# Feed-forward inputs of a fused transformer layer: normalised one step earlier and turned by transfers and VectorE

## What is computed

```python
x = x + LN(ffn(LN(x)))
# ffn: gu = x @ ternary(w_gate_up).T; gate, up = split(gu)
#      h = silu(gate) * up;  hn = h / sqrt(mean(h*h) + eps);  return hn @ ternary(w_proj).T
```

## Time and profile before

| | |
|---|---|
| median of 3 runs | 1040.49 us (1040.42 to 1040.52) |
| the profiled execution | 1039.91 us, span 1038.1 us |
| busy, share of the span | PE 98%, PEld 95%, DVE 80%, ACT 84%, POOL 90% |
| granted TensorE clock | 0.997 of full speed |
| transfers | 56 GB/s over the span, 17.2% of the 16 DMA engines' time |

### The profile page before, as it was taken

How to read it: one execution, slowest core, us unless ns; L and a number is a source line. 1 busy time by engine, 2 the same in 40 slices (tenths; PEclk the granted TensorE clock), 3 DMA queues, 4 the chain that set the end, 5 groups by cost and what they waited for, 6 DMA issues and landing times.

```text
span 1038.1 us, 25078 instructions
## 1 busy us (share of the span) xinstructions
PE 1021.4 (98%) x7827; PEld 981.6 (95%) x7827; DVE 827.1 (80%) x2841; ACT 868.2 (84%) x2399; POOL 931.4 (90%) x926
## 2 busy tenths in 40 slices
PE   7999999999999999999999999999999999999996
PEld 6899999999999999999999999999999999999996
DVE  6868888878887888788888888887777767677776
ACT  5988898989898989898989898889898867877774
POOL 4899999999999999999999999999999847877775
PEclk9999999999999999999999999999999999999998
DMA  7561121112112110121122112111131000000001
GB/s 262 187 184 43 42 63 41 43 52 68 44 36 61 63 42 33 62 63 42 33 68 67 42 39 75 43 42 53 42 113 31 2 1 11 22 24 29 22 22 41
DMA packets 35124, 58.56 MB, mean 56 GB/s; under 512 B 3136, under 2 KB 16000, under 8 KB 34688
## 3 DMA queue, kind: packets, MB, share of 16 engines
q1 hardware_dynamic: 34992, 56.96, 17.2%
HBM read 50.92 MB, written 9.18 MB: 58 GB/s over the span
## 4 chain that ended last, share of the span: by engine, by line
POOL 60%; PE 19%; issue 14%; DVE 1%; POOLq 0%; ACT 0%; ACTq 0%; DVEq 0%
POOL arena L599 15%; POOL arena L622 14%; POOL arena L633 13%; POOL arena L609 13%; PE psum L1017 12%; PE psum L1057 6%; POOL arena L581 1%; POOL arena L557 1%; POOL X L590 1%; PE psum L775 1%; PE psum L1030 1%; POOL arena L565 0%; PE psum L1039 0%; POOLq L303 0%; POOL arena L572 0%
## 5 line engine op out<-in xcount | busy, mean ns | idle before, releaser
L633 POOL TENSOR_TENSOR arena<-arena 128x768 f32<-128x768 f32 x128 | 196.2, 1533 | 8.9 <-DVE arena L1580 8.3
L609 POOL TENSOR_TENSOR arena<-arena 128x512 f32<-128x512 f32 x128 | 174.0, 1359 | 10.0
L1593 DVE SCALAR_TENSOR_TENSOR pt_split<-psum,vh_col,pt_split 128x256 fp32r<-128x256 f32 (+1 forms) x512 | 177.0, 407 | 3.5 <-ACT pt_split L1252 3.0
L599 POOL TENSOR_TENSOR arena<-arena,tables 128x512 f32<-128x512 f32 x128 | 166.9, 1304 | 13.7 <-ACT arena L1222 13.0
L622 POOL TENSOR_TENSOR arena<-arena 128x512 f32<-128x512 f32 x127 | 162.9, 1283 | 0.0
L929 PE MATMUL psum<-arena 128*128 128x256 f32 x512 | 153.9, 382 | 3.1 <-POOL arena L609 1.8
L775 PE MATMUL psum<-wo_hi,o_hi 128*128 128x256 f32 x512 | 152.1, 297 | 0.0
L1233 ACT ACTIVATE arena<-arena 128x256 f32<-128x256 f32 x256 | 128.6, 502 | 26.7 <-DVE arena L1570 20.1
L775 PE MATMUL psum<-xt_lo,wq_hi 128*128 128x256 f32 x512 | 144.7, 283 | 0.0
L775 PE MATMUL psum<-xt_hi,wq_lo 128*128 128x256 f32 x512 | 144.5, 282 | 0.0
L775 PE MATMUL psum<-wo_hi,o_lo 128*128 128x256 f32 x512 | 144.3, 282 | 0.0
(11 more groups left out here) (195 smaller groups left out, 3405.7 us busy)
## 6 DMA issues: line engine op xcount, KB each, us to landing
arena<-kh_rows SPq DMA_DIRECT2D x127, 256.0 KB, 3.3
out<-spare SPq DMA_DIRECT2D x15, 256.0 KB, 2.1
arena<-w_rows SPq DMA_DIRECT2D x6, 512.0 KB, 4.8
X<-L_attn_Wout SPq DMA_DIRECT2D x1, 2048.0 KB, 14.5
X<-L_attn_x SPq DMA_DIRECT2D x1, 2048.0 KB, 12.5
arena<-L_attn_Wq SPq DMA_DIRECT2D x1, 1536.0 KB, 10.0
X<-L_attn_x SPq DMA_DIRECT2D x1, 1536.0 KB, 9.7
w_rows<-L_ffn_w_gate_up SPq DMA_DIRECT2D x3, 512.0 KB, 8.2
```

Of the source, the lines that this page charges most:

```text
L599: nc.gpsimd.tensor_tensor(swap, swap, spread, ALU.mult).then_inc(q_sined, 1)
L609: nc.gpsimd.tensor_tensor(q_rot[p % 2], q_cos[p % 2], q_swap[p % 2], ALU.add).then_inc(q_roped, 1)
L633: nc.gpsimd.tensor_tensor(tb, tb, r.unsqueeze(3).to_broadcast([P, HP, 3, P]), ALU.mult).then_inc(p_ready, 1)
L1593: last = nc.vector.scalar_tensor_tensor(pt_lo[p % 2][:, o], b[:, i], vh[:, t, h:h + 1], pt_hi[p % 2][:, o].bitcast(F32), ALU.mult, ALU.sub ...
```

## The change

The normalising moves from a unit's second step to its first (FLAG norm=0), behind `square_hidden` 2 on ScalarE. TensorE's `turn_x2` goes for all units but unit 0. In its place SyncE issues four SBUF to SBUF transfers of 64 KB each, which spread the blocks over the partitions, and VectorE does one 32x32 block transpose of 128x512 float32 into F_BANK. ScalarE's `split_x2` moves ahead of `activate` 2, and VectorE's ahead of `stats_x2`, which itself stays in its step. SyncE's loop of stores is unrolled, and the transfers of unit u+4 stand behind the store of unit u. A new buffer `moved` of 2 KB in each partition is used.

```diff
-FLAG = dict(stats=0, norm=1, turn=1, up=2, sum=3, down=3, z=3, out=4)
+FLAG = dict(stats=0, norm=0, turn=1, up=2, sum=3, down=3, z=3, out=4)
+        moved = sb("moved", [P, NT * E])
+        by_rows = lambda rows, t: rows.rearrange("p t e -> p (t e)").rearrange("p (b k t c) -> p t k b c", b=4, k=ET, t=NT)[:, t]
+        by_blocks = lambda x_tile: x_tile.rearrange("p (k b c) -> p k b c", k=ET, b=4)
+        moved_in = moved[:, :].rearrange("p (a g c) -> p g a c", a=4, c=P // 4)
+        turned_out = F_BANK.rearrange("p (g q a) -> p g a q", a=4, q=P // 4)
...
 # SyncE
+            def spread_blocks(rows, landed):
+                flat = rows.rearrange("p t e -> p (t e)")
+                for b in range(4):
+                    sp.dma_start(moved[b * 32:(b + 1) * 32, :].rearrange("q (a g) -> q a g", a=4),
+                                 flat[:, b * P:(b + 1) * P]).then_inc(landed, 16)
...
-            with sp.Fori(0, BATCH - 3, 2) as u:
-                for i in range(2):
-                    rows = out_rows[:, bass.ds(address((u + i) * NT), NT), :]
-                    sp.wait_ge(res_done, u + i + 1)
-                    sp.dma_start(rows, res[i]).then_inc(stored[i], 16)
+            def move_x2(u):
+                sp.wait_ge(x2_norm, u * NT + NT)
+                sp.wait_ge(x2_turned, u)
+                spread_blocks(x2_rows(u, u % 2), x2_moved)
+            for u in range(1, 4):
+                move_x2(u)
+            for u in range(BATCH - 2):
+                sp.wait_ge(res_done, u + 1)
+                sp.dma_start(out_rows[:, u * NT:(u + 1) * NT, :], res[u % 2]).then_inc(stored[u % 2], 16)
+                if u + 4 < BATCH:
+                    move_x2(u + 4)
...
 # TensorE, step
                 at = unit_at(u0, s, FLAG["turn"])
-                if at and at[0] > 0:
-                    turn_x2(*at)
...
 # ScalarE, norm_x2
-                    nc.scalar.activation(x2_rows(u, i)[:, t, :], x_batch(u)[:, t, :], ACT.Identity, bias=x2_bias[:, t:t + 1],
+                    o, i_ = x2_rows(u, i)[:, t, :], x_batch(u)[:, t, :]
+                    if u > 0:
+                        o, i_ = by_rows(x2_rows(u, i), t), by_blocks(i_)
+                    nc.scalar.activation(o, i_, ACT.Identity, bias=x2_bias[:, t:t + 1],
...
 # VectorE
+            def turn_x2(u):
+                dve.wait_ge(x2_moved, u * 64)
+                dve.wait_ge(x2_lo_done, u)
+                nc.vector.transpose(turned_out, moved_in).then_inc(x2_turned, 1)
```

More of the change, by code:

```diff
@@ L284, in sandwich_kernel @@
         wgu_placed, wpr_placed = sem("wgu_placed"), sem("wpr_placed")
+        x2_moved = sem("x2_moved")
         x2_stats, x2_aggr, x2_eps, x2_neg, x2_inv, x2_biased, x2_norm, x2_turned, x2_hi_done, x2_lo_done = (
@@ L1338, in step @@
                     activate(*at, 1)
+                at = unit_at(u0, s, FLAG["up"])
+                if at:
+                    high_hidden(*at, 1)
+                    square_hidden(*at, 0)
+                    square_hidden(*at, 1)
+                at = unit_at(u0, s, FLAG["turn"])
+                if at and at[0] > 0:
+                    split_x2(*at)
+                at = unit_at(u0, s, FLAG["up"])
+                if at:
+                    activate(*at, 2)
+                    high_hidden(*at, 2)
+                    activate(*at, 3)
+                    square_hidden(*at, 2)
                 at = unit_at(u0, s, FLAG["norm"])
@@ L1343, in step @@
                 if at:
[L1344 to L1355, removed]
                     high_hidden(*at, 3)
@@ L1767, in step @@
                     multiply(*at, 1)
+                at = unit_at(u0, s, FLAG["turn"])
+                if at and at[0] > 0:
+                    turn_x2(at[0])
                 at = unit_at(u0, s, FLAG["z"])
@@ L1778, in step @@
                     multiply(*at, 2)
-                at = unit_at(u0, s, FLAG["turn"])
-                if at and at[0] > 0:
-                    split_x2(*at)
                 at = unit_at(u0, s, FLAG["z"])
```

## The result

The changed kernel takes **1067.67 us** (median of 6 runs, 1066.96 to 1071.67) against 1040.51 (6 runs, 1040.3 to 1040.53) before: ratio 1.0272, 95% interval 1.026 to 1.0283 (the two medians alone give 1.0261). It is slower by 27.2 us. The forecast was slower by 5.8 us, with a range that ended at 1054.5. The profiled execution took 1071.03 us around a span of 1069.2, 3.4 above the median. Its first norm_x2 starts at 766.55, where the kernel before has 763.92: its stream is 2.6 us late already ahead of the feed-forward part, and I take those 2.6 us out where I compare starts.

What follows compares the result with a forecast made beforehand. TensorE was taken to bound the kernel at 12.17 us a step, then a ring through SyncE at 12.85. Start +1.3, ten steps +6.8 and end -2.3 gave +5.8 us: 1046.3 us, range 1040.0 to 1054.5.

Steps and rivals of the forecast that it cites:

- What bounds before, and direction: Feed-forward part: TensorE alone sets the old step of 12.17 us; the change makes the kernel slower, chance 0.76.
- a ring through SyncE's queue: Blocked steps: transpose to add_x, store, four issues, landing, next transpose; 12.85 us a step (12.4 to 13.4), chance 65%.
- The new order at 12.28 us: ScalarE and VectorE: the moved operations need 12.28 us a step even with every transfer in time.
- The transpose at 0.70 us: VectorE: the new 32x32 block transpose takes 0.70 us, with bounds of 0.61 and 1.29.
- The rival of the dear transpose: VectorE: strided PSUM writes make the transpose take 1.3 us, the step 13.45 us and the total 1052.9 us; chance 14%.
- The ring inside the engines, 9.43 us: VectorE and GpSimd: from the start of the transpose to the end of add_x takes 9.43 us.
- The way through SyncE, 3.42 us: SyncE: from add_x through store, four issues and the fourth landing to the transpose takes 3.42 us (3.0 to 4.0).
- The early steps, "at nothing": Steps where SyncE's transfers are not behind a store: no net cost, TensorE's gain of 3 x 0.44 taken by the longer ring.
- The first blocked steps, +1.3: First steps with transfers behind a store: stats_z falls 1.3 us later, as leftovers of attention hold GpSimd anyway.
- The end, -2.3: Step after unit 15's transpose, without norm_x2, stats_x2 and invert_x2: about 9.8 us instead of 12.16, so -2.3 us.
- the transfers come in time: Rival: transfers land within 2.85 us of add_x, so ScalarE's and VectorE's order sets 12.28 us a step; 1039.8 us, chance 14%.
- TensorE stayed the bound: Rival: the engines' ring closes in under 11.73 us, so all 15 turns taken from TensorE are won; 1033.9 us, chance 7%.

Runs made afterwards that it cites:

- moves_first: The changed kernel with SyncE issuing the transfers of unit u+4 ahead of the store of unit u: 1044.99 us.
- stats_behind: stats_early with the four transfers put back behind the store on SyncE: 1061.55 us.
- no_moves: The changed kernel without its transfers; VectorE transposes the normalised rows where they lie, blocks not spread: 1044.14 us.
- split_back: moves_first with ScalarE's split_x2 back behind activate 2 and VectorE's back behind multiply 2: 1039.18 us.
- plain_moves: The changed kernel with its four transfers as plain copies of 32 rows of 2 KB to the same partitions, blocks not spread: 1065.09 us.
- stats_early: moves_first with the input's statistics a step earlier, norm_x2 back behind activate 1 and both split_x2 at their old places: 1035.86 us.
- stats_only: moves_first with only the input's statistics a step earlier (FLAG stats=-1), norm_x2 left at its late place: 1073.32 us.

## Why the prediction was wrong, step by step

**What bounds before, and direction.** Right. The time won on TensorE was lost to a ring through SyncE's queue; moves_first shows it by its removal, stats_behind by its return.

**The new order at 12.28 us.** Right: 12.27 in moves_first and 12.27 to 12.28 in no_moves, with high 2 idle 1.95 us. In split_back, where split_x2 is back, it is 11.9.

**The transpose at 0.70 us.** Right: 0.73, and its slot to stats_z 0.63 (954.91 to 955.54). The rival of the dear transpose falls, and with it the fear for a strided write: the Trainium skill, "SBUF — State Buffer", "Door 1: The DMA port swizzle", warns of non-contiguous access to PSUM for matmuls, and this write of VectorE at a stride of four elements takes 0.04 us more than VectorE's product of 128x512 (0.69).

**The ring inside the engines, 9.43 us.** Right: transpose to the end of add_x is 962.95 + 1.29 - 954.91 = 9.33 us in the base steps. In three steps (those from 897.36, 911.68 and 982.82) it was 9.6 to 9.8.

**The way through SyncE, 3.42 us. This is the term that failed, and the largest of the misses.** It takes 4.6 us (964.24 to 968.85), outside even my upper bound of 4.0:

| part | predicted | measured |
|---|---|---|
| store and three issues, to the start of the fourth | 1.80 | 2.39 (964.24 to 966.63) |
| landing of the fourth | 1.60 | 2.20 |

Both were read from the nearest rows, and in both the row was another kind of transfer. The 0.42 us came from output stores; an issue of this kind takes 0.60, and next to next 0.65 (965.33 to 965.99). For the landing I interpolated by size between 16 KB and 256 KB, but at 64 KB these land like the store of 256 KB (2.1), as does a single copy of 256 KB (2.4). The Trainium skill, "DMA: Bandwidth & Descriptors", "Anatomy of one DMA", gives a fixed cost of about 2.0 us for any size, for the GpSimd path. The prediction set it beside its 1.6 and did not take it; it stands closer to the 2.2 measured on SyncE's queue. In the landing it was the choice "nearer to the small one" that failed.

With 4.6 for 3.42, and 9.33 for 9.43, the step is 13.94 us instead of 12.85: 10.9 us more over ten steps. That alone lifts the forecast of 1046.3 to 1057.2, out of its range.

**Late landings, not foreseen.** The ten steps took 14.33 us on the mean and not 13.94. Some transfers land late. The chain shows it for the fourth ones:

```profile
893.84 3.50 DMA moved<-arena
...
951.61 3.27 DMA moved<-arena
```

The first of these came just ahead of the ten steps, the second within them, and a third of 3.77 at 1022.88, where the base steps have 2.20. In the stretch from the first issue (891.95) to the transpose (897.36), the DMA view has one packet of the instruction queue q8:

```profile
q8 instruction: 1, 0.02, 1.5%
```

So have the stretches of the other two late landings (from 949.73 and 1021.00), and the nine steps that landed in time have none; plain_moves shows the same split, three and nine. That such a packet holds the transfers up is likely by this, but no run tested it, and in stats_behind the way from add_x to the transpose at 890.92 has one and takes only 0.16 us more. The rest is in the three longer turns inside the engines. In that from 897.36, one small GpSimd instruction, the last of invert_z, is 0.64 us long, where it takes 0.26 in the base step, and it begins while VectorE's addition (L1725, 903.83 to 904.51) runs:

```profile
903.93 0.64 POOL L699 TENSOR_TENSOR arena<-arena 128x2 f32<-128x2 f32 x1
```

In all eleven turns from 881.75 to 1026.67 this instruction ends 0.05 to 0.07 us behind the end of that addition. The addition is late here because multiply 3 ahead of it is:

```profile
903.22 0.69 DVE L1710 TENSOR_TENSOR arena<-arena,psum 128x512 f32<-128x512 f32 x1 [0.43 <-PE psum L1039]
```

It waits for TensorE, whose granted clock had been at half from 900 to 903. The turn from 982.82 shows the same (clock at half from 986 to 988, multiply 3 at 5.96 us into the turn instead of 5.48, L699 0.73 us long). The turn from 911.68 has no low clock; there VectorE's second aggregate (L1768) begins 0.2 us late, without a wait that the profile shows.

The two late landings within the ten steps cost 1.1 and 1.6 us (5.68 and 6.17 behind add_x instead of 4.6), the three longer turns 1.1 together: 3.8 of the 3.9 us.

**The early steps, "at nothing".** Wrong, by 2.25 us. norm_x2 of unit 1 stands on ScalarE in the same step as its statistics, which the old FLAG did not ask for, and attention's last operations are queued behind it. ScalarE and VectorE of the changed kernel there:

```profile
838.58 1.09 ACT L1332 ACTIVATE arena<-X,arena 128x256 f32<-128x256 f32 x2 [3.90 <-POOL arena L686]
839.58 0.58 ACT L1281 ACTIVATE o_hi<-psum 128x512 fp32r<-128x512 f32 x1
```

```profile
840.18 0.69 DVE L1627 TENSOR_TENSOR o_lo<-psum,o_hi 128x512 fp32r<-128x512 f32 x1 [3.06 <-ACT o_hi L1281]
```

In stats_early, with the statistics a step ahead, ScalarE's wait at this place is 0.18 us. In moves_first the 2.25 us are there all the same (output statistics at 865.66, with a start 0.25 late): they do not come from SyncE's queue.

**The first blocked steps, +1.3.** Wrong: +7.5 in all up to the statistics at 898.00, of which 2.25 are the early steps and 5.2 two blocked steps that I had charged 0.35 and 0.95 (together the 1.3). The leftovers of attention did not cover for SyncE: the transpose of the first of them waits 2.00 us for its transfers like all others, and that of the second had a landing that came 1.3 late (5.93 us from add_x to transpose instead of 4.6).

**The end, -2.3.** Wrong: -0.67. I let the step without norm_x2 shrink to the ring's 9.8 us, and forgot that TensorE still has a unit to do in it. It took 1052.82 - 1041.32 = 11.50 us, with TensorE busy 11.43 of the 12 us from 1041 to 1053, as its own 11.73 a step foretold.

**The sum.** Against the forecast of +5.8 the span grew by 31.1. Of the 25.3 us between: 10.9 from the base step, which is the way through SyncE, 3.9 from late landings and longer turns, 6.2 up to the step of unit 6, 1.6 at the end, 2.6 in the start of this execution. The rivals fell as they should: in no blocked step did the transfers come in time, TensorE stayed the bound nowhere in that stretch, the transpose is cheap. But the forecast's own case had its top at a step of 13.4 us, and no landing in it was later than 2.1 us.

## What to carry to other kernels

A transfer that stands in a queue behind another's wait joins two units that have nothing to do with each other; here two lines in the other order are worth 22.7 us of 1067, and issuing one transfer in place of four brings the same time, in a run that leaves the spreading out. When a new transfer is priced, take issue and landing from rows of the same kind and count, let the landing's range reach well over the longest that the trace shows (2.2 us in the middle was 3.8 at the worst), and remember that a term in a ring is paid once a step. When a step is moved earlier, list for each of its buffers who must have read it: in stats_only a scale that exists once cost 28 us, in a place where no data was late.

## What of the hardware had not been expected

- An issue on SyncE of a transfer of 64 KB within SBUF, to 32 partitions, takes 0.60 us in the middle (0.55 to 0.72), whether it scatters pieces (0.602) or copies rows straight (0.590). One of 256 KB to all 128 partitions takes 0.47, and the store of 256 KB to memory 0.38. So the price does not go with the bytes; what it goes with is not settled (the number of partitions and their place were not tried apart).
- Landings of equal transfers in the same kernel went from 2.1 to 3.8 us. The three late ways among the twelve blocked steps are the three that have a packet of instruction queue q8 in them.
- A GpSimd instruction of 128x2 elements that runs beside a VectorE addition of 128x512 ended 0.05 to 0.07 us behind it in eleven of eleven steps, and took 0.25 to 0.73 us accordingly.
- A 32x32 block transpose of 128x512 float32 from SBUF to PSUM at a stride of four elements takes 0.73 us, next to 0.69 for VectorE's product of the same shape.
- The granted clock falls behind some of TensorE's idle times. The stretches of one step, columns as in the earlier trace rows:

```profile
954.00:955.00 1.00, 0.00 (x0) 0.00 (x0) 0.09 (x1) 0.00 (x0) 0.00 (x0) 1.00 0.01 2
...
956.00:957.00 1.00, 0.02 (x1) 0.02 (x1) 0.90 (x5) 0.75 (x2) 0.00 (x0) 1.00 0.00 0
957.00:958.00 1.00, 1.00 (x9) 1.00 (x10) 1.00 (x3) 0.00 (x0) 0.00 (x0) 0.99 0.00 0
958.00:959.00 1.00, 1.00 (x7) 1.00 (x6) 0.90 (x4) 0.00 (x0) 0.38 (x3) 0.50 0.00 0
...
962.00:963.00 1.00, 1.00 (x11) 1.00 (x10) 0.00 (x0) 1.00 (x3) 1.00 (x2) 1.00 0.00 0
```

  TensorE had worked next to nothing from 954 to 957 (0.02 us), behind the late landing; it started again at 1.00, and then ran at 0.50 of full speed, 1.2 GHz, from 958 to 961. The same followed the late landings of 893.84 and 1022.88, and one step with a common landing (986 to 988), but not the others. This makes the mean of 0.96. The turn inside the engines behind it was still 9.33 us: in that step the lower clock was hidden. It was not in the turns from 897.36 and 982.82, where VectorE's multiply 3 came late by it and the turn took 9.70 and 9.79 us: a dip costs nothing only as long as nobody in the chain waits for TensorE's next product.
